# Who writes the causal masks into the score banks of a decoder layer, and where the first probability quarter is turned

## The reference, cut to what matters

```python
qkv = jnp.einsum('bsd,de->bse', x, qkv_weights)     # 16 heads of 16
a = jnp.einsum('aib,ajb->aij', q, k) / scale
tril = jnp.tril(jnp.ones((S, S)))[None]
a = tril * a + NEG_INF * (1.0 - tril)               # NEG_INF = -1e9
a = jax.nn.softmax(a, axis=-1)
heads = jnp.einsum('aij,ajb->aib', a, v)
```

## Time and profile before

| what | us |
|---|---|
| median of 3 runs | 776.38 (776.12 to 778.15) |
| the profiled execution | 773.13 |
| its span, from the first to the last instruction | 771.3 |
| PE busy | 709.9 (92% of the span) |
| PE weight load busy | 533.2 (69%) |
| VectorE busy | 466.4 (60%) |
| ScalarE busy | 379.3 (49%) |
| GpSimd busy | 322.7 (42%) |

### The profile page before, as it was taken

How to read it: one execution, slowest core, us unless ns; L and a number is a source line. 1 busy time by engine, 2 the same in 40 slices (tenths; PEclk the granted TensorE clock), 3 DMA queues, 4 the chain that set the end, 5 groups by cost and what they waited for, 6 DMA issues and landing times.

```text
span 771.3 us, 20265 instructions
## 1 busy us (share of the span) xinstructions
PE 709.9 (92%) x5972; PEld 533.2 (69%) x5973; DVE 466.4 (60%) x1506; ACT 379.3 (49%) x1105; POOL 322.7 (42%) x451
## 2 busy tenths in 40 slices
PE   6988899999999999999997548999999999999993
PEld 5767788888888888888886314666666666665453
DVE  2543567778778777777766543444444444438984
ACT  0256677777777677777772202333333333312233
POOL 1001233235445445445556552555555555541111
PEclk9998999999999999999999868999999999999997
DMA  8644572213323323323344533422222222219862
GB/s 294 254 148 123 172 223 76 83 54 102 96 84 99 105 75 100 109 70 101 111 140 157 157 130 97 153 84 88 83 88 87 84 89 82 89 58 324 298 220 83
DMA packets 77035, 97.69 MB, mean 127 GB/s; under 512 B 12320, under 2 KB 63264, under 8 KB 75936
## 3 DMA queue, kind: packets, MB, share of 16 engines
q1 hardware_dynamic: 59920, 68.31, 28.2%
q0 software_dynamic: 6816, 19.00, 6.8%
q10 hardware_dynamic: 10224, 9.42, 4.5%
HBM read 60.12 MB, written 36.56 MB: 125 GB/s over the span
## 4 chain that ended last, share of the span: by engine, by line
PE 71%; issue 13%; DVE 5%; SPq 5%; DMA 3%; ACT 1%; POOL 1%; POOLq 0%; ACTq 0%; DVEq 0%
PE ps L991 16%; PE ps L1002 8%; PE ps L778 6%; PE ps L766 4%; PE ps L741 4%; PE ps L788 4%; PE ps L744 4%; PE ps L856 4%; PE ps L859 3%; PE ps L880 3%; PE ps L977 2%; DVE products L1253 2%; PE ps L984 2%; PE ps L866 2%; PE ps L917 2%
## 5 line engine op out<-in xcount | busy, mean ns | idle before, releaser
L1080 ACT ACTIVATE prob<-ps,nmax 128x128 f32<-128x128 f32 x512 | 143.0, 387 | 3.2 <-DVE nmax L1243 3.2
L991 PE MATMUL ps<-first_use,xgT 128*128 x284 | 135.5, 600 | 1.5 <-ACT xgT L1174 1.5
L1243 DVE TENSOR_REDUCE nmax<-ps 128x4 f32<-128x512 f32 x128 | 79.5, 683 | 72.0 <-PE ps L766 72.0
L1087 ACT COPY pT<-ps 128x512 f32<-128x512 f32 x128 | 77.6, 606 | 63.3 <-PE ps L778 62.8
L1461 DVE TENSOR_TENSOR hid<-ps,attn_only 128x512 f32<-128x512 f32 x71 | 49.1, 692 | 90.8 <-PE ps L991 89.7
L620 POOL TENSOR_TENSOR rot<-products 128x128 f32<-128x128 f32 x128 | 61.2, 500 | 82.3 <-DVE products L1253 82.2
L639 POOL DMA_INDIRECT sent<-packets,pos x64 | 63.5, 992 | 71.6 <-PE ps L766 57.2
L670 POOL TENSOR_TENSOR gate_h<-hid,sil 128x256 f32<-128x256 f32 x71 | 50.9, 716 | 97.1 <-DVE result_row L1474 82.6
L1174 ACT COPY xgT<-ps 128x256 f32<-128x256 f32 x71 | 26.4, 372 | 129.7 <-PE ps L977 124.0
L778 PE MATMUL ps<-tf,prob 128*128 128x128 f32 x512 | 80.1, 279 | 6.0 <-ACT pT L1087 6.0
L991 PEld LDWEIGHTS ps<-first_use,xgT 128*128 128x128 f32 x284 | 54.2, 192 | 40.4 <-issue 36.9
(11 more groups left out here) (133 smaller groups left out, 1334.5 us busy)
## 6 DMA issues: line engine op xcount, KB each, us to landing
xg<-sent ACTq DMA_DIRECT2D x68, 129.5 KB
first_use<-back SPq DMA_DIRECT2D x8, 1024.0 KB, 7.5
k_dram<-first_use SPq DMA_DIRECT2D x4, 1024.0 KB, 4.4
attn_only<-in_x_turned SPq DMA_DIRECT2D x32, 128.0 KB, 2.1
attn_only<-k_dram SPq DMA_DIRECT2D x256, 16.0 KB
attn_only<-in_x SPq DMA_DIRECT2D x32, 128.0 KB, 2.8
attn_only<-in_ctx SPq DMA_DIRECT2D x32, 128.0 KB, 2.7
first_use<-in_L_ffn_rw SPq DMA_DIRECT2D x8, 512.0 KB, 5.4
```

Of the source, the lines that this page charges most:

```text
L991: mm = eng.matmul(ps[:, r, :], xgT[:, r, c, :], rw1_sb[:, bass.ds(e * (DC * 2 * FFN) + c * 2 * FFN, 2 * FFN)], start=(c == 0), stop=(c == ...
L1080: ins = eng.activation(prob[:, t % 2, 4 * u + n, :], SCORE[u][:, n * P:(n + 1) * P], ACT.Exp, bias=nmax[:, t % 2, 4 * u + n:4 * u + n + 1])
L1087: eng.copy(pT[:, u, :, :].rearrange("p n t -> p (n t)"), PROBT).then_inc(pT_set, 1)
L1243: eng.tensor_reduce(nmax[:, t % 2, 4 * u:4 * u + 4], SCORE[u].rearrange("p (h j) -> p h j", j=P), AX_X, ALU.max, negate=True).then_inc(max ...
```

## The change: what it does

- The masks of sequence n+1 are written by `lay_mask(n + 1, u)` in step n: banks 1 and 2 by ScalarE, banks 0 and 3 by VectorE, each as one copy of the bf16 table (128 by 128, read four times over by a broadcast) into the whole bank, as soon as the bank's probabilities are made. `scores` waits for all four (`near_laid`, `far_laid`). PE writes the masks only once, before the first sequence, in four products of 128 by 512.
- MAX_ORDER goes from (3, 0, 1, 2) to (1, 0, 3, 2). From sequence 2 on, the maxima of the last bank are taken later in VectorE's step, behind the first norm's `add_eps`.
- ScalarE's step: the copy of PROBT's first quarter stands ahead of the heads' copy (L1094); the exponentials of bank 3 come before the last PROBT copy and those of bank 2 behind it; the copy x1T (L1137), which was the last of a step, stands ahead of mask 2 and of the queries' copy.
- VectorE's step: x1 and gc come ahead of the second norm's `bn_aggr` and `add_eps`, with the two masks between.
- PE: `turn_probs(n - 1, 0)` stands at the head of the step, ahead of `weigh` and `scores`.
- The bf16 table holds one mask instead of four rolled ones.

The diff, cut to its core:

```diff
-MAX_ORDER = (3, 0, 1, 2)
+MAX_ORDER = (1, 0, 3, 2)
...
-            def lay_masks(t):
-
-                after(eng, expd, 4 * t)
-                for a in range(4):
-                    for u in range(4):
-                        rows, lo = slice(32 * a, 32 * a + 32), (a + u) % 4 * 32
-                        eng.matmul(ps[lo:lo + 32, u, :].rearrange("p (h j) -> p h j", j=P), ident_bf[rows, rows],
-                                   causal_bf[rows, u, :].unsqueeze(1).broadcast_to([32, 4, P]), start=True, stop=False,
-                                   skip_group_check=True)
+            def lay_first_masks():
+
+                for u in range(4):
+                    eng.matmul(SCORE[u].rearrange("p (h j) -> p h j", j=P), ident_bf, causal_bf, start=True, stop=False,
+                               skip_group_check=True)
...
             def scores(t):
 
                 eng.wait_ge(q_set, t + 1)
                 eng.wait_ge(kp_in[t % 2], t // 2 * 128 + 128)
+                after(eng, near_laid, 2 * t)
+                after(eng, far_laid, 2 * t)
...
             def step(n):                        # PE
+                if n == 1:
+                    eng.wait_ge(kk_set, 13)
+                if live(n - 1):
+                    turn_probs(n - 1, 0)
                 if n == 2:
                     eng.wait_ge(kk_set, 4 * NG)
...
-                if n == 1:
-                    eng.wait_ge(kk_set, 13)
-                if live(n - 1):
-                    turn_probs(n - 1, 0)
...
-                if live(n + 1):
-                    lay_masks(n + 1)
+                if n + 1 == 0:
+                    lay_first_masks()
...
+            def lay_mask(t, u):                 # ScalarE
+
+                eng.wait_ge(expd, expd_count(t - 1, u))
+                eng.copy(SCORE[u].rearrange("p (h j) -> p h j", j=P), causal_bf).then_inc(far_laid, 1)
...
                 if live(n - 1):
                     out_probs(n - 1, 1)
+                if live(n) and live(n + 1):
+                    lay_mask(n + 1, 1)
+                if live(n - 1):
                     out_probs(n - 1, 2)
...
+            def lay_mask(t, u):                 # VectorE
+
+                eng.wait_ge(expd, expd_count(t - 1, u))
+                eng.tensor_copy(SCORE[u].rearrange("p (h j) -> p h j", j=P), causal_bf).then_inc(near_laid, 1)
...
                 if live(n):
-                    for u in MAX_ORDER:
+                    for u in MAX_ORDER[:3]:
                         maxes(n, u)
+                    if n < 2:
+                        maxes(n, MAX_ORDER[3])
```

More of the change, by code:

```diff
@@ L68, in shape_tables @@
     before = (i[:, None] < i[None, :]).astype(np.float32)
-    rolled = [np.roll(causal, -32 * u, axis=0) for u in range(4)]
-    bf = np.concatenate([ident, before, np.ones((P, P))] + rolled, 1)
+    bf = np.concatenate([ident, before, np.ones((P, P)), causal], 1)
     return np.ascontiguousarray(f32, np.float32), np.ascontiguousarray(bf, np.float32)
@@ L145, in decoder_kernel @@
         padding_end = tf[:, o + B:o + B + 3]
-        tb = sb("tb", [P, 7 * P], BF16)
+        tb = sb("tb", [P, 4 * P], BF16)
         before_bf = tb[:, P:2 * P]
@@ L149, in decoder_kernel @@
         ident_bf = tb[:, 0:P]
-        causal_bf = tb[:, 3 * P:7 * P].rearrange("p (u j) -> p u j", u=4)
+        causal_bf = tb[:, 3 * P:4 * P].unsqueeze(1).broadcast_to([P, 4, P])
         BH, BY = NE * 2 * FFN, NE * D
@@ L303, in decoder_kernel @@
         maxed = sem("maxed")
+        near_laid = sem("near_laid")
+        far_laid = sem("far_laid")
         expd = sem("expd")
@@ L1087, in out_probs @@
                 eng.copy(pT[:, u, :, :].rearrange("p n t -> p (n t)"), PROBT).then_inc(pT_set, 1)
+            def lay_mask(t, u):
+                eng.wait_ge(expd, expd_count(t - 1, u))
+                eng.copy(SCORE[u].rearrange("p (h j) -> p h j", j=P), causal_bf).then_inc(far_laid, 1)
             def step(n):
+                if live(n - 1):
+                    out_probs(n - 1, 0)
                 t = n - 2
@@ L1094, in step @@
                     eng.copy(oT[:, :, :].rearrange("p x t -> p (x t)"), ps[:, 5, :]).then_inc(oT_set, 1)
-                if live(n - 1):
-                    out_probs(n - 1, 0)
                 if live(n):
-                    exps(n, 3)
+                    exps(n, 1)
                 for q in groups_at(n, 1):
@@ L1119, in step @@
                 if live(n):
-                    exps(n, 1)
-                    exps(n, 2)
+                    exps(n, 3)
                 if live(n - 1):
                     out_probs(n - 1, 3)
+                if live(n):
+                    exps(n, 2)
+                t = n - 2
+                if live(t):
+                    eng.wait_ge(x1_turned, t + 1)
+                    after(eng, xq_made, t - 1)
+                    eng.copy(x1T[:, t % 2, :, :].rearrange("p c t -> p (c t)"), TR).then_inc(x1T_set, 1)
+                if live(n) and live(n + 1):
+                    lay_mask(n + 1, 2)
                 t = n + 1
@@ L1132, in step @@
                     eng.copy(va[:, t % 3, :, 0:DH], QV[:, D:2 * D].rearrange("p (h d) -> p h d", d=DH)).then_inc(v_set, 1)
[L1133 to L1137, removed]
             for n in range(FIRST_STEP, END_STEP):
@@ L1382, in step @@
                     add_eps(t2, mv1, mv1_set)
+                if live(n) and n >= 2:
+                    maxes(n, MAX_ORDER[3])
                 if live(t4):
@@ L1385, in step @@
                     eng.bn_stats(bn2[:, r4, :], res2[:, r4, :]).then_inc(bn2_set, 1)
-                    aggregate(t4, bn2, mv2, bn2_set, mv2_set)
-                    add_eps(t4, mv2, mv2_set)
                 if live(t2):
@@ L1396, in step @@
                     eng.tensor_tensor(gc[:, q % 2, t5 - GROUPS[q][0], :], GATE, gate_b_sb[:, 0:NE], ALU.add).then_inc(gc_set, 1)
+                if live(n) and live(n + 1):
+                    lay_mask(n + 1, 0)
+                if live(t4):
+                    aggregate(t4, bn2, mv2, bn2_set, mv2_set)
+                if live(n) and live(n + 1):
+                    lay_mask(n + 1, 3)
+                if live(t4):
+                    add_eps(t4, mv2, mv2_set)
                 if live(t4):
```

## The result

The changed kernel took 770.43 us (median of 20 runs: 19 of them took 767.07 to 775.48, and a disturbed one, at 1451.87, is left out of the ratio), the kernel before 775.91 beside it: ratio 0.994, 95% interval 0.9916 to 0.9963. The forecast was 772.7. So the gain is 0.4 to 0.8% by the first set, and between a loss of 0.2% and a gain of 0.4% by the second; the two sets differ by about as much as the effect. What follows goes by stretches of the traces, which repeat within 0.6 us in the middle of the loop. The whole of a trace is a poor guide here: the profiled executions of the changed kernel and of e1 (775.48 and 782.21 us) are the slowest of their sets, leaving out the disturbed run, and that of e4 (763.63) is the fastest of its set.

A forecast was written before the change was run, and what follows sets the result against it. PE was taken to bound the loop. A full step gains 0.37 - 0.02 - 0.03 - 0.10 = 0.22 us; 27 steps give 5.9, less 2.2 at the start: 3.7 us, so 772.7 us, range 770.5 to 775.

The forecast's parts named there:

- PE full: In the loop PE bounds the step; taking the masks off it gives at most 0.37 us in each of 27 steps.
- The turned quarter: On PE between L955 and the weighing: moving the quarter there costs 0.02 us a step, bounds 0 to 0.05.
- ScalarE's tail: x1T, mask 2 and queries' copy before the scores: 1.76 us, tying with PE's path; loss 0.03 us a step.
- VectorE's tail: Two masks, x1 and gc ahead of `add_eps` delay `packets` and the next maxima; loss 0.1 us a step.
- The third rival: VectorE becomes the bound, at the masks between gc and `packets`; slower from masks of 0.78 us; chance 0.18.
- The first rival: All covers hold, nothing gets late; a step gains 0.33 to 0.37 us, total 768.4 us; chance 0.20.
- The start: Step 0: VectorE's masks of sequence 1 behind the last key copy delay its scores; loss 2.2 us once, bounds 0 to 4.
- Behind the loop nothing changes: After the loop: no change in time, what follows hangs on the loop's end.

The follow-up runs named there:

- e1: The changed kernel run again unaltered, in another set: 775.22 us, ratio 0.9995 to the kernel before.
- e4: The changed kernel with both sequence 1's masks earlier on VectorE and VectorE's old order in steps without masks: 770.31 us, ratio 0.9919.
- e7: The kernel before with masks written once ahead of sequence 0, none in the loop: 766.42 us, ratio 0.9874, steps of 11.07 us.
- e5: The changed kernel with the first quarter turned behind the scores again: 786.22 us, ratio 1.0155.
- e10: The changed kernel with ScalarE's mask of bank 2 written twice: 784.51 us, ratio 1.014.
- e8: The changed kernel without the masks of ScalarE and VectorE in the loop: 773.43 us, ratio 0.9955, loop 291.7 us.
- e11: e4 with x1T again the last copy of ScalarE's step: 767.43 us, ratio 0.9908.
- e9: The changed kernel with VectorE's mask of bank 3 written twice: 777.37 us, ratio 1.0036.
- e2: The changed kernel with VectorE's masks of sequence 1 between its first and second key copy of step 0: 772.20 us, ratio 0.9968.
- e3: The changed kernel with VectorE's old order (second norm's aggregate and add_eps ahead of x1, gc) in steps without masks: 771.13 us, ratio 0.9939.
- e6: The kernel before with the turned quarter ahead of the weighing, masks still on PE: 786.13 us, ratio 1.0118.

## Why the prediction was right, point by point

- **PE full, the masks 0.37 us in 27 steps.** Right. e7 alone shows 11.44 to 11.07.
- **The turned quarter, 0.02 us.** L954 is left 0.09 us earlier (0.22 for 0.31), the turn takes 0.53 for 0.49, and L855 behind the scores 0.99 for 0.90: 0.04 us. With it 11.44 - 0.37 + 0.04 = 11.11, the shortest steps as measured.
- **ScalarE's tail, a tie, 0.03 us.** Right in mechanism and place (e5, e10). The tie itself cost PE nothing (e8); the place of x1T cost 0.05 us a step by e11, at L905 and not ahead of the scores. The mask took 0.596 us, a PROBT copy of the same size from PSUM 0.599, so the 0.045 us that the prediction weighed for a source in SBUF did not come.
- **VectorE's tail, 0.10 us.** Over-sized. The masks took 0.681 us, as assumed, and the wait ahead of `packets` grew from 0.37 to 0.67. But I set `packets` at 2.04 us behind L954, and it was 1.60. gc started 0.56 us ahead of L954 where I had it 0.43 ahead, from gc to `add_eps` it took 1.34 for 1.52, with the second aggregate between the masks, and from `add_eps` over the power to `packets` 0.82 for 0.95. So the maxima are 0.1 us late instead of 0.6, and e8 puts the cost of the masks at nothing. The third rival would have begun later too: e9 added 0.7 us for 0.19 a step. The first rival asked for masks under 0.6 us, some 0.4; the shortest took 0.669.
- **The start, 2.2 us.** Right at its place: 8.61 to 10.86 us from scores 0 to 1, and the cause by e2. Part came back behind it, where I expected none: from scores 1 to 3 the changed kernel takes 22.9 us for 24.9. To scores 5 the loss is 1.2 us in the first trace, 2.9 in e1, and in e3, with the same start, there is a gain of 0.9. With one trace of the kernel before, what is left of the 2.2 is not shown.
- **Behind the loop nothing changes.** Wrong; this term was put at nothing without a row. The steps without masks keep VectorE's new order, in which the power lies bare behind the gate: 2.1 us by e3 and e4, and with it, on the whole, a lower clock.

A step gained 0.28 us and not 0.22, and the tail lost 2.1 us in waits and 5.8 and 6.6 in the two traces: the sum of 3.7 us came out near the truth (5.5 and 1.4 us in two sets of runs) with two errors against one another. The mechanism of the loop was right; that the total fell so near was in part luck.

## What to carry to other kernels

Work moved off a full engine is worth its start-to-start time there, and is free elsewhere as long as it lies off the last hand-off: e7 against the kernel before shows the first, e8 against the changed kernel the second. Where a chain over two engines is made as long as the work that covers it, move cover and chain together (e5 against the change, e6 against the kernel before): one without the other loses. An order fitted to the steady step must be looked at again in the first and last steps, where the inserted work is missing and only the reordering is left.

## What the runs showed of the hardware

By the rows of e6 a change between whole and 32-wide products costs PE 0.05 to 0.1 us, and the place of one turn among the others was worth 0.19 us a step. A copy of 128 by 512 from bf16 in SBUF to PSUM took 681 ns on VectorE and 596 on ScalarE, where a copy of that size out of PSUM takes ScalarE 599: no 45 ns more for the SBUF source.
